# First steps of two convolutions at the head of a transformer kernel: the softmax exponential on GpSimd, the rank products later, the later filter bands from SP

## The reference, cut to what matters

```python
h = conv1d_grouped(x.T, conv1_w, conv1_b, c)      # 4 hidden channels for each of 256, 5 taps
h = gelu(h)                                       # exact gelu
h = conv1d_grouped(h, conv2_w, conv2_b, c)        # back to 256 channels, 5 taps
h = layernorm(h.T + x, ln0_g, ln0_b)
for i in range(4): h = linear_attention(h, ...)   # 4 layers
f = gelu(h @ W1 + b1) @ W2 + b2
x = layernorm(x + layernorm(f + h, ln2_g, ln2_b))
# second part: two weights composed from 32 of 64 primitives each
vals, idx = top_k(logits, 32); w = softmax(vals)
W = einsum('k,kir,kro->io', w, A[idx], B[idx])    # twice: W1 and W2
x = layernorm(x + gelu(x @ W1) @ W2)
```

## Time and profile before

| | |
|---|---|
| median of three runs | 1992.5 us (1987.11 to 1996.18) |
| the profiled execution, whole | 1988.1 us |
| its span on the core | 1986.4 us |
| mean granted PE clock | 0.982 of full |
| PE busy | 1921.8 us, 97% |
| DVE, POOL, ACT busy | 68%, 54%, 50% |
| end of the first stage (next stage's first PE work) | 192.56 us |

### The profile page before, as it was taken

How to read it: one execution, slowest core, us unless ns; L and a number is a source line. 1 busy time by engine, 2 the same in 40 slices (tenths; PEclk the granted TensorE clock), 3 DMA queues, 4 the chain that set the end, 5 groups by cost and what they waited for, 6 DMA issues and landing times. The chain is left out here.

```text
span 1986.4 us, 47561 instructions
## 1 busy us (share of the span) xinstructions
PE 1921.8 (97%) x19760; PEld 1577.8 (79%) x19760; DVE 1343.4 (68%) x3293; ACT 983.7 (50%) x1805; POOL 1073.3 (54%) x1000
## 2 busy tenths in 40 slices
PE   6998999999999999999999699999999999999998
PEld 2334878888888888888888478999999999999997
DVE  2555566766677666766677455768696968677776
ACT  3554567766676667766676454222223232223231
POOL 1444798999889998999889211212222121313221
PEclk8998999999999999999999899999999999999999
DMA  7343410122100300021001694101010001010100
GB/s 253 112 170 126 163 34 33 34 76 76 34 22 14 118 33 34 34 76 55 34 13 30 169 239 117 43 22 43 22 43 33 33 33 43 22 43 22 43 11 22
DMA packets 26247, 128.04 MB, mean 64 GB/s; under 512 B 4592, under 2 KB 5168, under 8 KB 19888
## 3 DMA queue, kind: packets, MB, share of 16 engines
q1 hardware_dynamic: 16912, 76.51, 11.5%
q0 software_dynamic: 4624, 34.67, 5.7%
q10 hardware_dynamic: 4496, 13.83, 1.8%
HBM read 93.53 MB, written 31.46 MB: 63 GB/s over the span
## 5 line engine op out<-in xcount | busy, mean ns | idle before, releaser
L29 PE MATMUL bankC<-down_hi,act_hi 128*128 128x256 f32 x1024 | 289.5, 283 | 0.0
L31 PE MATMUL bankC<-down_hi,act_lo 128*128 128x256 f32 x1024 | 287.0, 280 | 0.0
L30 PE MATMUL bankC<-down_lo,act_hi 128*128 128x256 f32 x1024 | 286.9, 280 | 0.0
L1453 DVE TENSOR_TENSOR act_lo<-gel,act_hi 128x512 fp32r<-128x512 f32 x256 | 210.6, 823 | 8.8
L29 PE MATMUL bankC<-aT_hi,up_hi 128*128 128x512 f32 x512 | 205.1, 401 | 1.4 <-DVE aT_lo L1442 1.4
L1415 POOL TENSOR_TENSOR rstdC<-var_epsC,minus_halfC 128x4 f32<-128x4 f32 x48 | 53.7, 1119 | 278.4 <-DVE var_epsC L1478 278.4
L31 PE MATMUL bankC<-aT_hi,up_lo 128*128 128x512 f32 x512 | 202.4, 395 | 0.0
L30 PE MATMUL bankC<-aT_lo,up_hi 128*128 128x512 f32 x512 | 201.5, 393 | 0.0
L30 PEld LDWEIGHTS bankC<-down_lo,act_hi 128*128 128x128 f32 x1024 | 192.9, 188 | 1.4
L29 PEld LDWEIGHTS bankC<-down_hi,act_hi 128*128 128x128 f32 x1024 | 192.8, 188 | 1.4
L31 PEld LDWEIGHTS bankC<-down_hi,act_lo 128*128 128x128 f32 x1024 | 192.7, 188 | 0.0
(11 more groups left out here) (195 smaller groups left out, 5408.8 us busy)
## 6 DMA issues: line engine op xcount, KB each, us to landing
w_first<-w_split POOLq DMA_DIRECT2D x8, 1536.0 KB, 7.1
w_second<-w_split POOLq DMA_DIRECT2D x8, 1536.0 KB, 8.2
xs<-in_x_conv SPq DMA_DIRECT2D x16, 513.0 KB, 6.6
u<-hA SPq DMA_DIRECT2D x8, 1024.0 KB, 4.6
u_next<-u SPq DMA_DIRECT2D x8, 1024.0 KB, 5.9
u<-yB SPq DMA_DIRECT2D x8, 1024.0 KB, 4.3
hC<-u SPq DMA_DIRECT2D x16, 512.0 KB, 3.9
xC<-in_x SPq DMA_DIRECT2D x16, 512.0 KB, 4.0
```

Of the source, the lines that this page charges most:

```text
L29: e.matmul(out, wh, xh, start=start, stop=False)
L30: e.matmul(out, wh, xl, start=False, stop=False)
L31: return e.matmul(out, wl, xh, start=False, stop=stop)
L1453: e.tensor_tensor(a_lo[:, fb, :], g, a_hi[:, fb, :].bitcast(F32), ALU.subtract).then_inc(s_act_lo, 1)
```

## The change

Five things are different.

1. The exponential leaves ACT. GpSimd computes it as `e` to the power of the shifted logit (`gpsimd_exp`, one `pow` on 64x2 elements), behind `edges(0)`; a constant tile `euler` is filled ahead of it.
2. ACT's loads stand in another order: `band1` part 0, first bias, `band2` part 0, the four ranking inputs, second bias, identity. The six later band parts leave ACT and are issued by SP between `load(0)` and the wait for the first gelus.
3. `rank.tensor` stands behind `conv2(0)` and writes into `back_ps` (the bank of the transposes) instead of `conv_ps`.
4. The waits for the identity and for DVE having emptied the ranking's bank move from the front of PE's loop and from step 1 into `to_tokens`.
5. On DVE the ranking's second half (`vector_rest`, from the copy out of PSUM on) stands in iteration 2, behind `add_input(0)`.

```diff
--- before.py
+++ after.py
@@ -1,3 +1,5 @@
+import math
+
 import concourse.bass as bass
 from concourse import mybir
 from contextlib import ExitStack
@@ -91,7 +93,7 @@
         s_conv, s_convT, s_back, s_y = (sem(n) for n in ("conv", "convT", "back", "y"))
         s_stats, s_mom, s_var, s_rstd, s_off = (sem(n) for n in ("stats", "mom", "var", "rstd", "off"))
         s_ln, s_ln_last = sem("ln"), sem("ln_last")
-        rank = Rank(nc, ctx, comp, tri, w_col, picks, conv_ps[:, 0:2 * P], conv_ps[:, 2 * P:4 * P])
+        rank = Rank(nc, ctx, comp, tri, w_col, picks, back_ps[:, 0, :], back_ps[:, 1, :])
         prep.allocate(nc, ctx, conv_ps)
 
         part = lambda t: (lambda a: [a[:, k * a.shape[1] // PARTS:(k + 1) * a.shape[1] // PARTS] for k in range(PARTS)])(t)
@@ -129,6 +131,9 @@
                                 h[:, b * TILES // 2:(b + 1) * TILES // 2, :].rearrange("p t c -> p (t c)")).then_inc(d_h[b], 16)
 
             load(0)
+            for k in range(1, PARTS):
+                e.dma_start(band1_parts[k], part(bands1)[k]).then_inc(d_band1[k], 16)
+                e.dma_start(band2_parts[k], part(bands2)[k]).then_inc(d_band2[k], 16)
             w.wait_ge(s_hidden, ROWS)
             load(1)
             prep.sync(e)
@@ -176,6 +181,8 @@
             for n in range(STEPS + LAG + 1):
                 if n < STEPS:
                     edges(n)
+                if n == 0:
+                    rank.gpsimd_exp(e)
                 for layer in prep.due(n, 0):
                     prep.gpsimd(e, layer)
                 q, half = half_at(n - 1)
@@ -230,38 +237,34 @@
                 m.then_inc(s_conv, 1)
 
             def to_tokens(n):
+                w.wait_ge(d_eye, 16)
+                w.wait_ge(rank.s_v, rank.ROW + 1)
                 w.wait_ge(s_convT, n + 1)
                 w.wait_ge(s_y, n)
                 for t in range(2 * MT):
                     m = e.transpose(back_ps[:, t, :], convT[:, n % 2, t * P:(t + 1) * P], identity[:, :])
                 m.then_inc(s_back, 1)
 
-            w.wait_ge(d_eye, 16)
             for n in range(STEPS + LAG):
                 if n < STEPS:
                     conv1(n)
-                if n == 1:
-                    rank.tensor(e)
-                    w.wait_ge(rank.s_v, rank.ROW + 1)
                 if 0 <= n - LAG < STEPS:
                     to_tokens(n - LAG)
                 if 0 <= n - 1 < STEPS:
                     conv2(n - 1)
+                if n == 1:
+                    rank.tensor(e)
             w.wait_ge(s_convT, STEPS)
             prep.tensor(e)
 
         def scalar(e):
             w = Waits(e)
             e.dma_start(band1_parts[0], part(bands1)[0]).then_inc(d_band1[0], 16)
+            e.dma_start(bias1[:, :], conv1_b).then_inc(d_bias1, 16)
+            e.dma_start(band2_parts[0], part(bands2)[0]).then_inc(d_band2[0], 16)
+            rank.scalar_loads(e)
+            e.dma_start(bias2[:, :], conv2_b).then_inc(d_bias2, 16)
             e.dma_start(identity[:, :], eye).then_inc(d_eye, 16)
-            e.dma_start(bias1[:, :], conv1_b).then_inc(d_bias1, 16)
-            rank.scalar_loads(e)
-            e.dma_start(band2_parts[0], part(bands2)[0]).then_inc(d_band2[0], 16)
-            e.dma_start(bias2[:, :], conv2_b).then_inc(d_bias2, 16)
-            rank.scalar(e)
-            for k in range(1, PARTS):
-                e.dma_start(band1_parts[k], part(bands1)[k]).then_inc(d_band1[k], 16)
-                e.dma_start(band2_parts[k], part(bands2)[k]).then_inc(d_band2[k], 16)
 
             def gelu(n):
                 cp, r = n % CP, n % 2
@@ -320,6 +323,8 @@
 
             rank.vector(e)
             for n in range(STEPS + LAG):
+                if n == LAG:
+                    rank.vector_rest(e)
                 if 0 <= n - LAG < STEPS:
                     keep_rows(n - LAG)
                 q, half = half_at(n)
@@ -354,7 +359,7 @@
         self.before, self.index = sb("before", [N, N]), sb("index", [N, 1 + K])
         self.more, self.same = sb("more", [N, 2, N]), sb("same", [N, 2, N])
         self.rank, self.top, self.expo = sb("rank", [N, 2]), sb("top", [N, 2]), sb("expo", [N, 2])
-        self.chosen, self.ones = sb("chosen", [N, 2]), sb("onesN", [N, P])
+        self.chosen, self.ones, self.euler = sb("chosen", [N, 2]), sb("onesN", [N, P]), sb("euler", [N, 2])
         self.weight, self.place = sb("weight", [N, 2, P]), sb("place", [N, 2, K])
         self.inv_sum, self.total, self.w_row = sb("inv_sum", [P, 2]), sb("total", [P, 2]), sb("w_row", [P, 2, K])
         sem = lambda n: ctx.enter_context(nc.semaphore("rank_" + n))
@@ -367,12 +372,14 @@
         e.dma_start(self.before[:, :], self.tri).then_inc(self.d_in, 16)
         e.dma_start(self.index[:, :], self.comp["index"]).then_inc(self.d_in, 16)
 
-    def scalar(self, e):
+    def gpsimd(self, e):
+        e.memset(self.ones[:, :], 1.0)
+        e.memset(self.euler[:, :], math.e).then_inc(self.s_ones, 1)
+
+    def gpsimd_exp(self, e):
+        e.wait_ge(self.s_ones, 1)
         e.wait_ge(self.s_v, self.LESS_TOP)
-        e.activation(self.expo[:, :], self.expo[:, :], ACT.Exp).then_inc(self.s_exp, 1)
-
-    def gpsimd(self, e):
-        e.memset(self.ones[:, :], 1.0).then_inc(self.s_ones, 1)
+        e.tensor_tensor(self.expo[:, :], self.euler[:, :], self.expo[:, :], ALU.pow).then_inc(self.s_exp, 1)
 
     LESS_TOP, PLACES, ROW = 9, 14, 15
 
@@ -401,6 +408,9 @@
             e.tensor_scalar(self.weight[:, f, :], self.ones[:, :], self.expo[:, f:f + 1], None, ALU.mult).then_inc(v, 1)
             e.tensor_scalar(self.place[:, f, :], self.index[:, 1:1 + K], self.rank[:, f:f + 1], None,
                             ALU.is_equal).then_inc(v, 1)
+
+    def vector_rest(self, e):
+        v, K, R = self.s_v, self.K, P // 2
         e.wait_ge(self.s_mm, 1)
         e.tensor_copy(self.w_row[:, :, :].rearrange("p a b -> p (a b)"), self.rows_ps[:, 0:2 * K]).then_inc(v, 1)
         e.tensor_copy(self.picks[:, :], self.picks_ps[0:1, 0:2 * K]).then_inc(v, 1)
```

## The result

The changed kernel took 1982.23 us in the median of six runs (1980.46 to 1984.03), the kernel before 1991.8 us in the six runs beside them. The ratio is 0.9953 with a 95% interval of 0.9937 to 0.9968, so 6.4 to 12.5 us were won. The same change run once more, in another group of runs, gave 1983.75 against 1990.11, a ratio of 0.9972 (0.9957 to 0.9987), which is 5.6 us. The two intervals overlap, and the 7.5 us that were forecast lie between the two gains, 9.4 and 5.6 us by the ratios. The profiled execution took 1980.46 us, 7.6 less than the profiled one of before.

A forecast was written before the change was run, and what follows sets the result against it. PE, busy 97% of the span, was held by late starts in the first 40 us. The smaller of the PE and weights paths gave about 8 us; half a microsecond off made 7.5, so 1985.0 us, range 1979 to 1991.

The forecast's parts named there:

- Start of PE: PE's first matmul, no longer waiting for the identity, starts at 6.5 us, 1.7 us sooner.
- First gelu: ACT is free at about 8 us, so the gelu waits for `conv1(0)` until 10.9, 6.7 us sooner than 17.57.
- PE to step 2: `conv1(2)` starts sooner than 28.29: 7.1 us won at the lower clock level (1.2 GHz), about 10 at the upper (2.4).
- The power: GpSimd's `pow` on 64x2 takes 1.0 us, between 0.20 and 1.68, hidden from all but the ranking chain.
- Ranking inputs: The ranking loads land 0 to 5.6 us later than 11.59, taken as 2.8, so `place` is ready at 18.2.
- the late end: Ranking inputs 5.6 us later, `place` ready at 21.7 at the latest; could give back up to 3.5 us of 10.
- the sum: The smaller of the gains over PE (7.1 to about 9.3 us) and over the weights (7.8 to 9.3): about 8.
- The bands on SP: SP ends issuing the six band loads at about 5.4 us; they delay nothing on SP and their landing is hidden.
- Attention weights: `w_raw` is issued at 16.2 and lands at 24.3 to 25.8, limiting the gain to 7.8 to 9.3 us.
- Handing on: Later stages begin from the first one's end, the next at 192.56 before, and are moved whole, 7 to 9 us sooner.
- The slower rival: PE's wait at the ranking drops the clock to 1.2 GHz; 4.4 us per full step, four steps give 2002; chance 0.06.
- the 0.5% that was given 0.69: Measured time within 0.5%, 10 us, of the kernel before: chance 0.69; faster than that 0.27, slower 0.04.

The follow-up runs named there:

- early table load: The changed kernel with one gelu on a 128x1 tile ahead of `gelu(0)`, waiting for nothing late: 1983.07 us, ratio 0.9965 to the kernel before.
- bands experiment: The changed kernel with the six later band parts back on ACT, behind its nine loads: 1981.43 us, ratio 0.9958 to the kernel before.
- seven powers: The changed kernel with six more powers of the same size on GpSimd ahead of the real one: one run, 1983.3 us.
- all three: The changed kernel with a tiny early gelu, DVE's `w_parts` behind `add_input`, and layer 0's `w_raw` ahead of `load(1)`: 1975.37 us, ratio 0.9928 to before.

## Why the prediction was right, point by point

- **Start of PE.** Forecast 6.5, measured 6.59. With the identity first it was 7.94. Right.
- **First gelu.** Forecast 10.9, measured 11.68. The step was mis-sized by two terms that partly cancel. The table load costs 1.3 us: I had it done by 8 us, in ACT's idle time, as the exponential's had been (6.64 us, before), but the gelu's stood behind the gelu's wait. And the first gelu's input was there at 10.38, 0.5 us sooner than 10.9: I had taken the end of a group of 68 matmul records for the end of `conv1(0)`, but `conv1(0)` is 64 of them, and the gelu needs only the first of its banks. With an early table load the gelu came at 10.67. The term's direction and size (5.9 of 6.7 us) held; the experiment with the exponential on ACT gives 3.8 us of it to that one wait, and the bands experiment none to the bands themselves.
- **PE to step 2.** Forecast 18.5 to 22, measured 19.55, 19.37 in the repeat. The path was worth 8.7 us, between the 7.1 of the lower level and the 10 of the upper. The level changed at 16.5 us, behind most of `conv1(1)` (4.38 us) and ahead of `conv2(0)` (1.93).
- **The power.** I took 1.0 us, it took 0.69. Hidden, with 2.2 us to spare, as seven of them showed.
- **Ranking inputs.** I took them 2.8 us late, within 0 to 5.6; they came 0.8 us late (12.41 for 11.59). The bands experiment gives 0.3 to 0.5 us of it to SP's longer burst. By the Trainium skill, "DMA: Bandwidth & Descriptors", "Queues, rings and completion order", the DMA engines take turns between queues, and I had written that this speaks for the late end; the trace agrees in the direction, but 0.8 of 5.6 us is near the early one. This step was too pessimistic, and it cost the sum nothing, since PE came for the places at 18.6 anyway.
- **The bands on SP.** I had SP done issuing them at 5.4 us; it was 6.7, and nothing waited for it.
- **Attention weights.** Forecast: GpSimd at 24 to 26, released by a DMA. Measured: 25.30, released by `w_raw`. It was issued at 16.97 (forecast 16.2, late with the gelus) and took 8.1 us to land, as before. This was the step that limited the gain, as the sum had it (7.8 to 9.3; measured 8.31 at the transposes), and the early table load shows it as a hard limit: an earlier PE gained nothing. With the weight issued first and DVE's order changed as well, it did.
- **Handing on.** I wrote that the stages behind are moved whole. In the profiled execution the next stage's first work moved by 6.4 us only and the span by 7.8. Forecast were 7 to 9 us for the first. The step missed that PE's bias products become last when the level falls early among them. The repeat of the change shows the size, 1.9 us. That the span still came out at the forecast 8 us is luck in this execution: ACT's issues in the next stage happened to be 1.4 us shorter. In the repeat neither happened, and the first matrix product came 8.3 us sooner, as the span did.
- **The slower rival** had the right mechanism (PE waits, the level falls, steps run at 1.2 GHz) in the wrong places. One was the wait for the weights and not that for the ranking, which reached 1.77 us with seven powers and left the level where it was. It showed in two experiments, where the weight came late for PE, lasted about 7 us and cost 2.6 to 2.8. The other was ahead of everything I had looked at: the stop of 1.35 us behind `conv1(0)`, after which the level fell in the changed kernel itself, from 13.1 to 16.5 us. Neither made the kernel slower than before.

The gain forecast for the median, 7.5 us, came out as 9.4 (6.4 to 12.5) and 5.6 (2.6 to 8.6), and both measured ratios are within the 0.5% that was given 0.69. What separates executions of one kernel by several us is only partly settled: the moment at which the level changes differs and has a price at each place shown above, but I haven't accounted for a whole run's spread with it.

## What to carry to other kernels

Follow a wait in a queue to everything that stands behind it: here a 0.2 us exponential held six loads, a table load, the first gelus, and through them PE and all later transfers. When such a start is shortened, look at once for the transfer whose issue hangs on an unchanged event, because an engine that arrives early at it stops longer, and TensorE's stop of 3.29 us cost it the upper clock level and 2.8 us, more than had been won. A table load can stand behind the wait of the instruction that first uses the function, as that of the gelu did; one tiny use of the function, early, moves it into idle time.

## What the runs showed of the hardware that I had not expected

- A table load can wait with its instruction: ACT was idle from 6.6 to 10.38 us and loaded the gelu's table only then, for 1.28 us. The exponential's table was loaded at 6.64 us, before and with the exponential back on ACT, while the exponential itself waited until 13.43 and 13.98. In the code one wait stands directly ahead of the exponential and two ahead of the first gelu; whether that makes the difference, no run shows.
- During PE's stops of 3.29 and 3.52 us, in two executions, the level fell to 1.2 GHz for 6.8 us (from 31.2 and 33.7 us); stops of 1.08 to 1.51 us at the same place left it. Early in the kernel it was otherwise: in six executions the level was granted at 9.7 to 12.0 us, PE stopped for 1.35 to 1.42 us between `conv1(0)` and `conv1(1)`, and at 13.1 to 15.4 us the level fell. Without that stop (early table load, all three) it stayed.
- The group of 68 records that holds `conv1(0)` took 4.36 us and more wherever it was seen apart (64 records take 2.35 at the upper level). The level first rose at moments between 9.7 and 22.3 us; in two executions of the changed kernel it was 9.7 and 15.8.
- GpSimd's power on 64x2 took 0.69 us, less than the 1.01 on 128x4.
- While PE worked on the one-column products at the end of the stage, the level fell, 0.9, 3.6 and, before, 4.1 us after the first of them had started, although PE is recorded as busy throughout.
